# Sixteen-head attention: a pipeline's first steps placed three slots earlier

## What is computed

```python
x = x + attention_0(layernorm(x))          # one head, 128 wide
x = x + moe_0(layernorm(x))                # shared experts (1024 wide) + 8 routed, top 2, with a capacity
x = x + attention_1(layernorm(x))          # 16 heads of 8, below
x = x + moe_1(layernorm(x))                # 8 experts, top 1

def attention_1(x, W_in, b_in, W_out, b_out):
    q, k, v = heads(x @ W_in.T + b_in)     # 16 heads, D = 8
    bias = minimum((i - j) * slope[h], 8.0)
    p = softmax(q @ k.T / sqrt(8) + bias)
    return join(p @ v) @ W_out.T + b_out
```

## Time and profile before

| | us |
|---|---|
| median of 3 runs | 874.59 |
| lowest, highest | 870.59, 879.38 |
| profiled execution | 867.89 |
| its span | 866.1 |
| busy in it: PE, DVE, POOL, ACT | 758.6, 493.8, 459.6, 415.1 |
| first score of the sixteen heads | 415.6 |
| mean granted clock of PE | 0.941 of full speed |

### The profile page before, as it was taken

One profiled execution on the slowest core, in us unless ns is written; L12 is line 12 of the kernel. 1 busy time (PEld: TensorE's weight loads), 2 busy tenths in 40 slices (PEclk: granted clock), 3 DMA queues, 4 the chain that ended last, 5 costly groups with the idle time before them and its releaser, 6 DMA issues.

```text
span 866.1 us, 18067 instructions
## 1 busy us (share of the span) xinstructions
PE 758.6 (88%) x5344; PEld 529.2 (61%) x5344; DVE 493.8 (57%) x1800; ACT 415.1 (48%) x1023; POOL 459.6 (53%) x821
## 2 busy tenths in 40 slices
PE   4787989999965999997889999999999898559994
PEld 3676836666634777745365566656565454359994
DVE  4877474332210323333777888888888673356662
ACT  3466232222121323224336687777687567336662
POOL 4411306777772424243436556878678365525662
PEclk9999699999987999999998999999999899669997
DMA  9999996111111332221855645565544400712220
GB/s 241 203 236 197 196 194 150 45 39 39 44 35 46 97 114 90 66 64 48 138 110 105 112 99 100 118 116 104 111 101 89 76 16 5 243 41 62 60 58 13
DMA packets 102941, 87.05 MB, mean 101 GB/s; under 512 B 8158, under 2 KB 93361, under 8 KB 100701
## 3 DMA queue, kind: packets, MB, share of 16 engines
q1 hardware_dynamic: 96444, 74.58, 43.0%
q0 software_dynamic: 5600, 11.12, 4.0%
q10 hardware_dynamic: 816, 0.39, 0.3%
HBM read 43.65 MB, written 42.00 MB: 99 GB/s over the span
## 4 chain that ended last, share of the span: by engine, by line
PE 50%; POOL 16%; DMA 12%; issue 9%; DVE 7%; ACT 4%; POOLq 1%; ACTq 0%; DVEq 0%; SPq 0%
PE bank L1941 5%; PE bank L1757 5%; PE bank L1892 5%; DMA xg_rows<-arena,send_slot 5%; DMA arena<-arena 4%; PE bank L1809 4%; PE bank L1920 4%; PE bank L1758 4%; PE bank L2064 3%; POOL arena L838 3%; PE bank L2074 3%; POOL xg_rows L718 2%; DMA out_x<-arena 2%; PE bank L1710 2%; PE bank L1833 2%
## 5 line engine op out<-in xcount | busy, mean ns | idle before, releaser
L1499 ACT ACTIVATE arena<-bank 128x512 f32<-128x512 f32 x256 | 151.6, 596 | 51.6 <-PE bank L1920 21.1
L1118 DVE TENSOR_TENSOR arena<-arena,bank 128x320 f32<-128x320 f32 (+1 forms) x112 | 64.2, 573 | 175.1 <-ACT arena L1469 174.8
L1469 ACT ACTIVATE arena<-bank 128x320 f32<-128x320 f32 (+1 forms) x112 | 56.5, 506 | 172.3 <-PE bank L1758 172.3
L1214 DVE CUSTOM_DVE_ANT_0 rt<-bank,alibi 128x256 f32<-128x256 f32 x288 | 109.5, 421 | 19.6 <-PE bank L1892 16.6
L1920 PE MATMUL bank<-arena 81*128 81x256 bf16 x512 | 105.9, 280 | 11.8 <-DMA arena<-arena 9.3
L1892 PE MATMUL bank<-arena 72*128 72x256 bf16 (+1 forms) x512 | 101.3, 280 | 5.7 <-DVE arena L1214 4.1
L1757 PE MATMUL bank<-arena 128*128 128x320 f32 (+1 forms) x224 | 99.9, 528 | 2.4 <-DVE arena L1118 2.4
L838 POOL TENSOR_TENSOR arena<-arena 128x234 f32<-128x234 f32 (+2 forms) x192 | 83.8, 468 | 27.5 <-ACT arena L1499 27.4
L1758 PE MATMUL bank<-arena 128*128 128x320 f32 (+1 forms) x224 | 95.5, 508 | 0.0
L1209 DVE TENSOR_REDUCE arena<-bank 128x2 f32<-128x512 f32 x112 | 76.5, 689 | 28.0 <-PE bank L1892 27.4
L1941 PE MATMUL bank<-arena 128*32 128x256 f32 x1024 | 84.4, 404 | 0.0
(11 more groups left out here) (278 smaller groups left out, 1461.8 us busy)
## 6 DMA issues: line engine op xcount, KB each, us to landing
sorted_rows<-empty_row SPq DMA_DIRECT2D x1, 16896.0 KB, 110.2
arena<-qk_parts SPq DMA_DIRECT2D x60, 192.0 KB
qk_parts<-arena SPq DMA_DIRECT2D x16, 384.0 KB, 2.8
back_rows<-empty_row SPq DMA_DIRECT2D x1, 4096.0 KB, 36.8
arena<-back_rows SPq DMA_DIRECT2D x16, 256.0 KB, 2.8
arena<-in_w SPq DMA_DIRECT2D x2, 2048.0 KB, 11.1
arena<-qk_parts SPq DMA_DIRECT2D x30, 128.0 KB
xg_rows<-empty_row SPq DMA_DIRECT2D x1, 2580.0 KB, 25.7
```

The lines of the kernel that those rows point to most:

```text
L1214: last = nc.vector.tensor_tensor_reduce(biased[n % 2 * QT + u], bank[n % 2][:, SEQ * u:SEQ * u + SEQ], alibi[:, h, P * (1 - u):P * (1 - u) ...
L1499: nc.scalar.activation(prT3[:, n % PR].rearrange("p k t -> p (k t)"), bank[2 + n % 2][:], ACT.Exp).then_inc(exp3_done, 1)
```

## The change

Fourteen of the offsets are lowered by three: combine, statistics, variance, root, the two halves of the norm, output bias, turn, its copy, the query and key projection, their two copies and their parts. `VALUE` (-25) and `VALUES` (-21) stay. Chunks of the shared experts move along: chunk 8 four slots sooner, chunk 11 six slots sooner (ahead of the first score), 9 and 10 nearly where they were, 12 to 15 unchanged. `LATER_ADD` of the first group goes from -18 to -23. The down products stay. No function changes, and no instruction is added or taken away.

```diff
--- before.py
+++ after.py
@@ -65,16 +65,16 @@
 
 
 EXP_LAG = 25
-COMBINE_0, COMBINE_1, STATS, VARIANCE, ROOT, NORM_0, NORM_1, OUTPUT_BIAS = -42, -41, -38, -37, -36, -34, -33, -29
-TURN, HT, QK, Q_COPY, K_COPY, PARTS_QK, VALUE, VALUES = -32, -31, -27, -26, -25, -24, -25, -21
+COMBINE_0, COMBINE_1, STATS, VARIANCE, ROOT, NORM_0, NORM_1, OUTPUT_BIAS = -45, -44, -41, -40, -39, -37, -36, -32
+TURN, HT, QK, Q_COPY, K_COPY, PARTS_QK, VALUE, VALUES = -35, -34, -30, -29, -28, -27, -25, -21
 SPLIT_MAX_0, SPLIT_MAX_1, TURN_MAX, COPY_MAX, SEND_MAX = NH + 1, NH + 2, NH + 4, NH + 5, NH + 6
 LATER_FIRST = 8
-LATER_GATE = {8: -20, 9: -8, 10: -6, 11: 0, 12: 1, 13: 6, 14: 9, 15: 12}
-LATER_UP = {8: -20, 9: -8, 10: -6, 11: 0, 12: 3, 13: 8, 14: 10, 15: 13}
-LATER_SILU = {8: -19, 9: -8, 10: -6, 11: -3, 12: 1, 13: 6, 14: 9, 15: 12}
-LATER_PRODUCT = {8: -19, 9: -8, 10: -4, 11: 0, 12: 4, 13: 9, 14: 11, 15: 14}
+LATER_GATE = {8: -24, 9: -8, 10: -7, 11: -6, 12: 1, 13: 6, 14: 9, 15: 12}
+LATER_UP = {8: -24, 9: -8, 10: -7, 11: -6, 12: 3, 13: 8, 14: 10, 15: 13}
+LATER_SILU = {8: -23, 9: -8, 10: -7, 11: -6, 12: 1, 13: 6, 14: 9, 15: 12}
+LATER_PRODUCT = {8: -22, 9: -8, 10: -7, 11: -6, 12: 4, 13: 9, 14: 11, 15: 14}
 LATER_DOWN = [{-25: (1, 2, 3)}, {15: (0,), 17: (1,), 18: (2,), 19: (3,)}]
-LATER_ADD = [-18, 20]
+LATER_ADD = [-23, 20]
 FACTOR, WEIGH_0, WEIGH_1, KEEP = EXP_LAG + 2, EXP_LAG + 6, EXP_LAG + 7, EXP_LAG + 8
 BACK = NH - 1 + KEEP + 1
 TURN_0, DIVIDE_0, TURN_1, DIVIDE_1 = BACK, BACK + 2, BACK + 3, BACK + 4
```

## The result

The changed kernel takes 891.7 us (median of 4 runs, 888.45 to 897.54), the kernel before 877.0 on the same occasion (870.59 to 879.43): a ratio of 1.022, interval 1.017 to 1.027. That ratio compares fast executions alone; the two medians as they stand are 14.7 us apart and give 1.017. It is slower, by 15 to 19 us, where 872 and at most 884 were forecast. The profiled execution of the changed kernel took 888.45 us (span 886.7) against 867.89 (866.1). The 20.6 us between the spans lie in the stage of the 256 heads: from its first score to its last it takes 317.0 us instead of 298.8, and the first score comes at 418.56 instead of 415.56. After the last score both need the same (151.1 and 151.7 us). Counted from the first combine, which is free of what ran before the stage, to the last score it is 345.0 us instead of 322.1: 22.9 us more.

What follows compares the result with a forecast made beforehand. PE's own order of work was taken as the bound, with long stretches from maxima transfers waiting behind reads. 867.9 - 14.9 - 3.0 + 0.8 + 7 + 6.3 + 1 = 865.1 us profiled, given as 872 for the median, range 857 to 884.

Steps and rivals of the forecast that it cites:

- the ACT step: ACT: first norm three slots sooner waits for POOL's root in three batches; 6.3 us lost, plus 1 for the clock.
- Rival C: First norm waits for POOL's root three times, each followed by half clock (3 us); 880 us, chance 0.15.
- Rival D: Maxima late for another reason than the reads; transfer not cleared, only the losses come; 890 us, chance 0.12.
- Moved at no cost: Query and key projection from slot 5 to 2, covered by PE's order; also copies, turn and output bias; nothing summed.
- The DVE step: DVE: combines three slots sooner delay the fifth row maximum; 0.7 us in each of ten batches, 7 us lost.
- The transfer step: POOL's parts and SP's reads three slots sooner, so the maxima transfer no longer waits; 14.9 us gained.
- The start: Start of the 256-head stage: half clock behind 453 goes, 3.0 us gained; row maxima start later, 0.8 us lost.

Runs made afterwards that it cites:

- the sends spread: Two sends in slots 0 and 2 of one batch, two in the next, instead of four in one: changed kernel ratio 1.005, kernel before 0.999.
- the turn behind the score: Changed kernel with batch 2's turn and its copy alone at slots 0 and 1, behind the first score: ratio 1.026.
- the projection alone: Kernel before with only the query and key projection on PE three slots sooner (slot 2 instead of 5): ratio 1.010.
- the combine alone: Kernel before with only both combines, the statistics and the variance three slots sooner: ratio 1.003.
- the sends behind the root: Changed kernel with the sends of sorted rows on POOL five slots later (slots 9 to 12 instead of 4 to 7): ratio 1.026.
- with the chunks back: Changed kernel with chunks 8 to 11 of the shared experts and the first addition where they were before: ratio 1.029.
- keys alone: Kernel before with query and key projection, their copies and the parts three slots sooner, all else staying: ratio 1.009.
- both kernels without sends: Changed kernel and kernel before with all sends held back until the last batch is through: 903.5 and 897.65 us, one run each; stages 293.4 and 289.2 us.

## Why the prediction was wrong

**Two steps failed.** The first is the ACT step, by its size. Its mechanism was right: the places (batches 7, 9 and 11), the instruction (L1514 for POOL L797) and what is queued behind it were as described. It was priced at 6.3 us and 1 for the clock. The stage with four sends in slots 4 to 7 is 23.3 us longer than with the sends spread; 19.5 of them lie in the stretches of batches 7, 9 and 11 (16.8) and 8 (2.7), which the step speaks of. Four things were missed.
- The parts were put 5.9 us after the batch's first score (589.1 against 583.2). They start at 7.4 us (601.47 against 594.1), since the keys they split are copied late, and POOL idles 1.60 us for them with three sends behind it. The root ended 16.8 us into the batch, not 15.5. The waits of L1514 came to 9.9 us in three, 3.3 each, where 2.1 was counted as PE's stall.
- The stall does not end with the wait. The gaps between scores 12 and 16 of these batches summed to 9.5 us against 4.0 with the sends spread: norm, values and exponential queue up on ACT, the row maxima behind them on DVE, and then the turn on PE.
- After these stalls the clock fell to 1.2 GHz, for 13.7 us from 565.0, 3.4 from 612.8 and 6.8 from 653.8. Rival C had this and the point from which it decides (3.4 us a time) but put it at 0.15 and at 3.0 us a time. C had the mechanism, at 880 us. D's 890 is nearer in number, but its reason fell (below): that is chance.
- Late signals of PE share these stretches and no step of the prediction has them. Of the rest of the 23.3 us, 3.5 in the last stretch (a signal 2.5 us late, 3.4 us of half clock) and 1.1 in that of batch 13 are theirs, where no root is waited for. How much of the 19.5 is theirs isn't known: the queue alone made these stretches as long in the kernel with the turn behind the score, and late signals alone did in the kernel with the projection alone.

**Moved at no cost** was the second failure. The projection was held to be covered by PE's order, as PE was busy 17.40 of 17.40 us. But taking its 0.9 us out of slot 5 gave back 0.34, since PE then waited for ACT, and DVE was idle for 0.04 of 1.31 us there in batch 6; putting it in slot 2 cost all of it. Shares of busy time don't tell the two slots apart (DVE was idle for 0.08 of 1.11 us in slot 2); only moving the work did. Where no late signal stands, the projection alone makes a stretch 18.2 to 18.4 us instead of 17.4 (17.8 in batch 4): 0.8 to 1.0 us, in each of some ten stretches, where nothing was counted.

**The DVE step** was right by itself (the combine alone: 0.7 us in the gap it was forecast for, 0.7 forecast; 1.0 and 1.2 in stretches 4 and 6), but it does not add to the projection: each alone makes a stretch about 18.2 to 18.8 us, and both together 18.2 to 18.5. While PE is late by the projection, DVE has room for the combine: the gap from score 4 to 5 is 1.26 us in the changed kernel, as before. Forecast for quiet stretches was 17.9 to 18.2, measured 18.2 to 18.5.

**The transfer step** was right in its mechanism. The waits of L1920 for a DMA vanished, and the first packet of each maxima transfer left 1.4 us after its issue, but for the first two. Its size is not shown. With the sends spread, stretches 8, 10, 12 and 14 of the changed kernel sum to 74.9 us against 83.7 before; but the kernel before with its sends spread has 74.6 there, without any earlier key. So much of the late transfer came from the sends ahead of the parts, and both cures win the same time. Rival D fell. It followed from the rule of the Trainium skill ("DMA: Bandwidth & Descriptors", Queues, rings and completion order) that queue rows take turns, by which a small transfer should not mind the reads; here it minded them: it took 5.01 and 6.38 us beside late reads the earlier trace rows, and in the changed kernel, with the reads over, PE waited for none.

**The start.** The half clock after 453 went (20.4 to 17.9 us: 2.5 gained for 3.0 counted). Against it, from the first combine to the 17th score is 46.4 us instead of 43.0: 3.4 lost for 0.8 counted. Moving the turn of batch 2 back returned 2.6 of the 4.7 us by which the first score is later, but 0.4 of the 3.4 at the 17th. Part of the 3.4 comes and goes with the clock: the kernel with the sends behind the root has the same start and took 44.8 us, at full clock where the changed kernel's was halved from 418.3 to 421.7. What holds the rest was not found.

**The sum.** With the sends spread the changed kernel is within 0.5% of the kernel before (1.005), where the prediction without its ACT step would have stood at 0.988. By the profiles, from the first combine to the last score takes 322.4 us with the sends spread and 322.1 before, where the sum without the ACT step wants 10 less. So by the profiles 10 of some 26 us of error lie in projection, start and transfer together and the larger part in the sends. By the timed runs, taken on two chips, it is the other way round: 15 of 22 us lie there and 7 in the sends. That both parts failed is shown; which is the larger is not.

## What to carry to other kernels

Where an in-order queue serves two consumers, count for each consumer what stands ahead of its item at the moment it is asked, including the time the queue stands idle on an earlier item; moving one item three slots earlier put three sends between a split and a root, and the wait behind them cost more than the late transfer it cured. Moving the whole burst of four elsewhere made no kernel with the early keys as fast as the one before; splitting it in two came within 0.5%. When one cure leaves the time as it is, look whether another fault has taken its place: the sends behind the root ended the wait and were as slow for late signals. An engine that is full all through a stretch does not make its order free: work can leave a slot for next to nothing, where another engine is as late, and cost its full time in the slot it goes to. Only the gaps between the scores, not the busy shares, told the two slots apart.

## What the runs showed of the hardware

In six of the kernels matmuls were answered late while a send was running on POOL or just after it. In the example, from the changed kernel near 724 us, DVE and ACT stand idle for 2.58 and 2.07 us with finished matmuls before them; rows of PE, DVE, ACT and POOL:

```profile
723.86 0.39 PE L1892 MATMUL bank<-arena 72*128 72x256 bf16 x2
724.09 0.38 PE L1920 MATMUL bank<-arena 81*128 81x256 bf16 x2
...
727.01 0.42 DVE L1214 CUSTOM_DVE_ANT_0 rt<-bank,alibi 128x256 f32<-128x256 f32 x1 [2.58 <-remote]
...
726.79 0.60 ACT L1499 ACTIVATE arena<-bank 128x512 f32<-128x512 f32 x1 [2.07 <-PE bank L1920]
...
724.83 0.95 POOL L848 DMA_INDIRECT sorted_rows<-xw,slot  x1 [0.30 <-issue]
```

```
kernel                          scores over 0.5 us late   longest, us
changed kernel                        10                    2.5
with the chunks back                  10                    2.3
sends behind the root (9 to 12)       16                    2.5
combine alone                          9                    2.8
keys alone                             9                    2.3
projection alone                      10                    3.1
before, and all the others             0                     -
```

In each of the six they form five spells, in the stretches of batches 7, 9, 11, 13 and 15, all beside or within 1.4 us after a send. An idle DVE began 0.24 to 0.29 us after a late signal, as after any other (median 0.25).

That sends are needed is likely, since both kernels without sends show none. They are not enough: the kernel before, and the one with the turn behind the score, which has the changed kernel's sends in the same slots, show none. The latter is as slow as the changed kernel, so late signals are not needed for its long stretches; the kernel with the projection alone, where no root is late, has such stretches with late signals alone. Whether the matmuls themselves or only their signals were late can't be told, since the ends of matmuls are modelled in these records; why PE stood still is open.

How long a stall of PE is did not tell how long the half clock behind it lasts. In the changed kernel the granted clock fell to 1.2 GHz at 565.0, between waits of PE of 0.78 and 1.66 us, for 13.7 us; at 612.8, behind waits of 1.54 and 0.90, for 3.4; at 653.8, within a wait of 3.56, for 6.8. With the sends behind the root it fell at 691.9, behind a wait of 1.86, for 20.5. Other stalls had none behind them: in the kernel with the keys alone the 16 stretches stayed at 2.4 GHz throughout, with 28 waits of up to 1.9 us on PE between 450 and 737.
